# Queries and keys spread over partitions by DMA, and Newton inverse roots replaced by a power instruction on GpSimd, in a fused attention and expert layer

## The reference

```python
qg, kv = split_heads(ln(x) @ Wqg, 16), split_heads(ln(x) @ Wkv, 16)
queries, gates = qg[..., :16], qg[..., 16:]        # 16 key dims, 64 value dims per head
keys, values = kv[..., :16], kv[..., 16:]
queries, keys, values = l2norm(queries), l2norm(keys), l2norm(values)
attn = square(relu(queries @ keys^T))
out = tanh_norm(attn @ values) * tanh(silu(gates))
x = x + out @ Wout
x = x + moe(ln(x))      # 16 experts of 64, top 2 of 4 groups, top 4, and a shared expert
```

## Time and profile before

| what | value |
|---|---|
| median of the runs | 889.2 us |
| the profiled execution: its time, its span | 892.35 us, 890.6 us |
| PE busy | 753.3 us, 85% |
| DVE busy | 687.8 us, 77% |
| ACT busy | 512.4 us, 58% |
| POOL busy | 414.9 us, 47% |
| granted TensorE clock, mean | 0.944 |

### The profile page before, as it was taken

The page is one execution under the profiler, slowest core; times in us unless marked ns, Lnnn a source line. Parts: engine busy times, 40 slices in busy tenths (PEclk is TensorE's granted clock), DMA queues, the critical chain, the costliest instruction groups (busy, mean ns, idle before and its releaser), DMA issues.

```text
span 890.6 us, 17912 instructions
## 1 busy us (share of the span) xinstructions
PE 753.3 (85%) x5440; PEld 586.3 (66%) x5440; DVE 687.8 (77%) x2012; ACT 512.4 (58%) x1112; POOL 414.9 (47%) x395
## 2 busy tenths in 40 slices
PE   3787788889989888988988889898888898887876
PEld 2554557767766766766666677767677676765666
DVE  5767767888787878878788887878778887868654
ACT  4766466566656656666665666665665666643201
POOL 3474555464544645553455555445364645444000
PEclk9889799999999999999999999999999999999877
DMA  7000000000000000000000000000000000000000
GB/s 175 7 1 6 1 7 1 1 14 1 13 1 13 1 8 6 0 12 0 13 0 12 0 0 13 0 12 0 13 0 0 12 0 7 2 7 1 7 7 7
DMA packets 15988, 8.56 MB, mean 10 GB/s; under 512 B 5040, under 2 KB 15664, under 8 KB 15920
## 3 DMA queue, kind: packets, MB, share of 16 engines
q1 hardware_dynamic: 15920, 7.82, 3.3%
HBM read 5.72 MB, written 2.10 MB: 9 GB/s over the span
## 4 chain that ended last, share of the span: by engine, by line
PE 45%; DVE 42%; issue 8%; ACT 4%; POOL 1%; DVEq 1%; POOLq 0%; ACTq 0%
PE ps_a L464 8%; PE ps_f L328 7%; PE ps_f L330 5%; PE ps_f L329 5%; PE ps_f L408 5%; DVE norms_y L639 4%; DVE norms_t L638 4%; DVE ln_t L638 4%; PE ps_s L435 3%; PE ps_f L385 3%; DVE norms_t L637 3%; DVE it L850 3%; DVE it L832 3%; DVE ln_y L639 2%; DVE ln_t L637 2%
## 5 line engine op out<-in xcount | busy, mean ns | idle before, releaser
L295 POOL TENSOR_TENSOR p<-r 128x512 f32<-128x512 f32 x256 | 265.5, 1058 | 390.9 <-ACT r L577 390.9
L577 ACT ACTIVATE r<-ps_s 128x512 f32<-128x512 f32 x256 | 139.0, 599 | 37.2 <-PE ps_s L435 31.7
L464 PE MATMUL ps_a<-p,v 128*64 128x256 f32 x1024 | 147.3, 402 | 5.1 <-POOL p L295 4.5
L544 ACT ACTIVATE qkt<-ps_f 128x512 fp32r<-128x512 f32 x128 | 75.6, 599 | 42.9 <-PE ps_f L362 34.6
L569 ACT ACTIVATE it<-ps_f 128x256 f32<-128x256 f32 x144 | 56.1, 390 | 68.5 <-PE ps_f L330 66.8
L464 PEld LDWEIGHTS ps_a<-p,v 128*64 128x64 f32 x1024 | 64.7, 139 | 45.4 <-issue 6.4
L305 POOL TENSOR_TENSOR qks<-qk,qks 128x512 fp32r<-128x512 f32 x64 | 82.3, 1308 | 13.8 <-DVE qks L720 13.8
L832 DVE TENSOR_TENSOR it<-ps_f,it 128x256 f32<-128x256 f32 x144 | 58.7, 423 | 32.7 <-ACT it L569 25.4
L408 PE MATMUL ps_f<-wdown,it 128*128 128x128 f32 x576 | 75.7, 289 | 8.3 <-DVE it L850 8.3
L880 DVE TENSOR_TENSOR big<-ps_a,wt 128x256 f32<-128x256 f32 x128 | 52.1, 417 | 39.1 <-ACT big L586 27.4
L408 PEld LDWEIGHTS ps_f<-wdown,it 128*128 128x128 f32 x576 | 71.7, 204 | 15.2 <-issue 10.6
(11 more groups left out here) (152 smaller groups left out, 1732.3 us busy)
## 6 DMA issues: line engine op xcount, KB each, us to landing
x_in<-in_L_attn_tokens SPq DMA_DIRECT2D x16, 128.0 KB, 2.2
out<-o_sb SPq DMA_DIRECT2D x16, 128.0 KB, 1.8
big<-in_L_attn_Wqg SPq DMA_DIRECT2D x1, 640.0 KB, 3.8
big<-in_L_attn_Wkv SPq DMA_DIRECT2D x1, 640.0 KB, 5.1
big<-in_L_ffn_w_gate SPq DMA_DIRECT2D x1, 512.0 KB, 6.8
big<-in_L_ffn_w_up SPq DMA_DIRECT2D x1, 512.0 KB, 4.8
wout<-in_L_attn_Wout SPq DMA_DIRECT2D x1, 512.0 KB, 4.8
wdown<-in_L_ffn_w_down SPq DMA_DIRECT2D x1, 512.0 KB, 5.7
```

The costliest lines, as they stand in the source:

```text
L295: pool.tensor_tensor(p[h % 4][:], r[h % 2][:], r[h % 2][:], ALU.mult).then_inc(probs_done, 1)
L464: last = pe.matmul(ps_a[k % 2][64 * e:64 * e + 64, 0:N], v[q][:, t, h * DV:(h + 1) * DV], p[h % 4][:, t * N:(t + 1) * N], start=(t == 0), ...
L544: act.activation(qkt[pq][:, j, :], ps[:], ACT.Copy).then_inc(read[kind], 1)
L577: act.activation(r[h % 2][:], ps_s[h % 2][:], ACT.Relu).then_inc(relu_done, 1)
```

## The change

The transposes `tr`, the tile `qks` and its four writers are gone. The projections of queries and keys now have the weights as the stationary side, so that they come out transposed, with dims on partitions: 2 jobs of 2 x 3 matmuls with 256 columns in place of 2 jobs of 3 with 512. ScalarE writes their high part and their squares, VectorE their low part (`low_parts`, one instruction a job in place of L712 and L720), into `qk_parts` (1 MB). SyncE stores that tile to a DRAM buffer with one DMA, waits for it, and fills `qkt` (2 MB) with 12 loads, each of which writes 16 partitions; scores of pair 0 wait for all of them (`qk_loaded`). SyncE's steps are written out instead of looped over. The squares are summed per head by four more matmuls in the job `ones` (with `head16`), and `nT` turns 48 columns instead of 16; this replaces two of the six reductions L731. The last squares and sums of v (`sums(3)`) lie at the end of slot 1.

Both Newton roots become one instruction on GpSimd each, `tensor_tensor` with `ALU.pow` and an exponent tile of -0.5: for the norms, now 128 x 64, in slot 2 behind the pair's squares; for the layer norms, 128 x 4, in slot 6 behind the scaling of v. The inverse squares of query and key norms are VectorE reciprocals of 128 x 32. VectorE waits for the first root (`norms_ready`) ahead of `gate_up([5])`, and in slot 3 the order is head scales, value scales, `gate_up([6, 7])`, the gated heads, `gate_up([8])`. `FILL` is written anew. In step 17 `gate_up([0, 1, 2])` stands ahead of the route scores. GpSimd builds five more constant tiles or parts of them at the start.

```diff
-        [("P", "qk", 0), ("P", "qk", 1), ("P", "v", 0), ("O", "ones", 0), ("P", "v", 1), ("P", "v", 2)],
-        [("F", "gu", 0), ("P", "v", 3), ("O", "nT", 0), ("F", "lg", 0), ("F", "gu", 1), ("F", "gu", 2)],
-        [("F", "gu", 3), ("F", "gu", 4), ("F", "gu", 5), ("F", "gu", 6), ("F", "gu", 7)],
-        [("P", "g", 0), ("P", "g", 1), ("F", "gu", 8), ("P", "g", 2), ("O", "rT", 0)],
-        [("O", "rB", 0), ("P", "g", 3), ("O", "rB", 1), ("P", "tr", 0), ("O", "rB", 2), ("P", "tr", 1), ("O", "rB", 3),
-         ("P", "tr", 2)],
-        [("O", "y", 0), ("O", "y", 1), ("P", "tr", 3), ("F", "cT", 0), SKIP],
-        [("F", "cB", 0), ("P", "tr", 4), ("F", "cB", 1), ("P", "tr", 5), ("F", "cB", 2), ("P", "tr", 6), ("F", "cB", 3),
-         ("P", "tr", 7), SKIP],
+        [("P", "qk", 0), ("P", "v", 0), ("P", "qk", 1), ("P", "v", 1)],
+        [("F", "gu", 0), ("N", "ones", 0), ("P", "v", 2), ("F", "gu", 1), ("N", "nT", 0), ("P", "v", 3)],
+        [("F", "gu", 2), ("F", "lg", 0), ("F", "gu", 3), ("F", "gu", 4), ("F", "gu", 5)],
+        [("F", "gu", 6), ("F", "gu", 7), ("P", "g", 0), ("F", "gu", 8), ("O", "rT", 0)],
+        [("O", "rB", 0), ("P", "g", 1), ("O", "rB", 1), ("O", "rB", 2), ("P", "g", 2), ("O", "rB", 3)],
+        [("O", "y", 0), ("O", "y", 1), ("F", "cT", 0), SKIP],
+        [("F", "cB", 0), ("F", "cB", 1), ("P", "g", 3), ("F", "cB", 2), ("F", "cB", 3), SKIP],
...
+            def store_qk(b, q):
+
+                wait(sp, qk_loaded[q], (b - q) * (QK_LOADS // 2))
+                rows = qk_rows[q].rearrange("(l p) n -> p l n", p=P)
+                sp.dma_start(rows, qk_parts[:].rearrange("p l a c n -> p (l a c) n").bitcast(F32))\
+                  .then_inc(qk_stored[q], 16)
+
+            def load_qk(q):
+
+                rows = qk_rows[q].rearrange("(l a k e d) n -> l a e d k n", l=2, a=2, e=2, d=DK)
+                both = qk_rows[q].rearrange("(l m e d) n -> l e d m n", l=2, e=2, d=DK)
+                for e in range(2):
+                    for slot in range(4):
+                        at = 64 * e + DK * slot
+                        dst = qkt[q][at:at + DK, :, :, :].bitcast(F32)
+                        lq, lk = slot // 2, slot % 2
+                        if lq == lk:
+                            sp.dma_start(dst.rearrange("p a k n -> p (a k) n"), both[lq, e]).then_inc(qk_loaded[q], 16)
+                        else:
+                            sp.dma_start(dst[:, 0], rows[lq, 0, e]).then_inc(qk_loaded[q], 16)
+                            sp.dma_start(dst[:, 1], rows[lk, 1, e]).then_inc(qk_loaded[q], 16)
...
+                if "P" in on:
+                    b, pq = s + 1, 1 - q
+                    sp.wait_ge(read["qk"], 2 * b + 2)
+                    store_qk(b, pq)
+                    sp.wait_ge(qk_stored[pq], (b - pq) * 8 + 16)
+                    wait(sp, scores_done, 16 * (b - 1))
+                    load_qk(pq)
...
+            def root(tiles, ready):
+
+                y = tiles["y"][:]
+                pool.tensor_tensor(y, tiles["m"][:], minus_half[:].broadcast_to(y.shape), ALU.pow).then_inc(ready, 1)
+
+            def norm_roots(s, on):
+                if "P" in on:
+                    pool.wait_ge(sums_done, 4 * s + 8)
+                if "N" in on:
+                    pool.wait_ge(read["nT"], s + 2)
+                root(nt, norms_ready)
+
+            def ln_roots(s, on):
+                if "L" in on:
+                    pool.wait_ge(ch_l, 3 * (s + 3))
+                if "O" in on:
+                    pool.wait_ge(ch_n, 3 * s)
+                root(ln, ln_ready)
...
+                    if k == 2 and on & {"P", "O"}:
+                        norm_roots(s, on)
+                    if k == 6 and on & {"L", "O"}:
+                        ln_roots(s, on)
...
-                    last = three(ps[:, 0:2 * HK], (xh[:, tok[j]], xl[:, tok[j]]), (wqk[0][:], wqk[1][:]))
+                    for c in range(2):
+                        cols = slice(j * HK + c * P, j * HK + (c + 1) * P)
+                        last = three(ps[:, c * N:(c + 1) * N], (wqk[0][:, cols], wqk[1][:, cols]), (xh[:], xl[:]))
...
                 elif kind == "ones":
-                    pe.wait_ge(a2_done, 8 * b + 8)
-
-
-                    for a in range(2):
-                        for c in range(4):
-                            last = pe.matmul(ps[32 * c:32 * c + 32, 0:N], ones32[:, a, :], a2[:, 4 * a + c, :],
-                                             start=(a == 0), stop=(a == 1))
+
+                    sums = []
+                    if "O" in on:
+                        pe.wait_ge(a2_done, 8 * (s - 1) + 8)
+                        for a in range(2):
+                            sums.append([(ones32[:, a, :], a2[:, 4 * a + c, :]) for c in range(4)])
+                    if "P" in on:
+                        pe.wait_ge(qk_squared, 2 * (s + 1) + 2)
+                        sums.append([(head16[:], qk_sq[:, c // 2, c % 2, :]) for c in range(4)])
+                    for i, tiles in enumerate(sums):
+                        for c, (which, squared) in enumerate(tiles):
+                            last = pe.matmul(ps[32 * c:32 * c + 32, 0:N], which, squared,
+                                             start=(i == 0), stop=(i == len(sums) - 1))
...
-                    pe.wait_ge(read["tr"], 8 * b + 8)
+                    pe.wait_ge(qk_loaded[q], (b - q) * (QK_LOADS // 2) + QK_LOADS)
...
-                    act.activation(qk[:, j, :], ps[:, 0:2 * HK], ACT.Copy).then_inc(read[kind], 1)
+                    whole = ps[:].rearrange("p (c n) -> p c n", n=N)
+                    act.activation(qk_parts[:, 0, j, :, :], whole, ACT.Copy)
+                    wait(act, done["ones"], b)
+                    act.activation(qk_sq[:, j, :, :], whole, ACT.Square).then_inc(qk_squared, 1)
...
+            def low_parts(j, b):
+
+                dve.wait_ge(qk_squared, 2 * b + j + 1)
+                dve.tensor_tensor(qk_parts[:, 1, j, :, :], bank[("qk", j)][:].rearrange("p (c n) -> p c n", n=N),
+                                  qk_parts[:, 0, j, :, :].bitcast(F32), ALU.subtract).then_inc(read["qk"], 1)
...
                     if k == 2:
                         for c in range(3):
-                            if P_on or O:
-                                newton(link_norms, nt)
                             if F:
-                                gate_up([3 + c])
+                                gate_up([2 + c])
                             if c == 1:
                                 gated_heads(k)
-                        if F:
-                            gate_up([6])
+                        if P_on or O:
+                            dve.wait_ge(norms_ready, s + 2)
                         if O:
                             head_norms(link_o, b, rq2[pq])
                         if F:
-                            gate_up([7])
+                            gate_up([5])
                     if k == 3:
                         if O:
...
+                        if F:
+                            scale_hidden([0, 1, 2, 3])
                         if L_on or O:
-                            seed(link_ln, ln)
-                        if F:
-                            scale_hidden([0, 1])
-                        if L_on or O:
-                            newton(link_ln, ln)
-                        if F:
-                            scale_hidden([2, 3])
-                        if L_on or O:
-                            newton(link_ln, ln)
-                            newton(link_ln, ln)
-                            link_ln.end()
```

More of the change, by code:

```diff
@@ L258, in step @@
                       .then_inc(out_stored, 16)
-            run_steps(sp, step)
+            for s in range(FIRST_STEP, LAST_STEP + 1):
+                step(s, s % 2, stages(s), s)
             sp.wait_ge(out_stored, 16 * B)
@@ L297, in step @@
                         b = s + 1
-                        if k in (1, 2):
-                            t = k - 1
-                            wait(pool, done["tr"], 8 * b)
-                            for part in range(2):
-                                pool.wait_ge(qk_hi[t], 2 * b + part + 1)
-                                hi, lo, whole = slots_of(part, t)
-                                pool.tensor_tensor(lo, whole, hi.bitcast(F32), ALU.subtract).then_inc(qk_lo, 1)
                         if k in (4, 5, 6, 7):
@@ L495, in expert_weights @@
                 act.activation(weu[0][:], big[:, base + FC * P:base + 2 * FC * P], ACT.Copy).then_inc(w_hi, 1)
-            def high_parts(t, s):
-                b = s + 1
-                wait(act, done["tr"], 8 * b)
-                act.wait_ge(read["qk"], 2 * b + t + 1)
-                for part in range(2):
-                    hi, _, whole = slots_of(part, t)
-                    act.activation(hi, whole, ACT.Copy).then_inc(qk_hi[t], 1)
             def gates(j, s, q):
@@ L530, in evacuate @@
```

(34 more changed lines are left out.)

148 lines of the change are left out of this document (62 added, 86 removed).

## The result

The changed kernel takes 992.65 us (median of 4 runs, 991.79 to 993.01) where the kernel before takes 889.38 beside it (886.67 to 891.09): a ratio of 1.117, 95% interval 1.114 to 1.121. It is slower by 103 us. The forecast was 798.

A forecast was written before the change was run, and what follows sets the result against it. TensorE's own queue, interrupted by five waits, was taken to bound the full step: 51.1 us falling to 45.5, 73 us in 13 steps. With the other steps the sum was -91 us, 798 against 889.2; range 776 to 860.

The forecast's parts named there:

- I take 3 us for the norms (nearer the rows): GpSimd's power on 128 x 64 for the norm root: 3 us, chosen between estimates of 2.6 and 10.6.
- hidden up to 4.4 us: Norm root in slot 2: up to 4.4 us hidden before ScalarE's tanh; above that each microsecond costs one a step.
- `rT`: TensorE's wait at the end of slot 3, behind evacuation, tanh, scales and `gate_up` 6: a new wait of 2.2 us.
- `cT`: TensorE's wait for the routing chain: grows from 0.89 us by 1.1, as less TensorE work lies between.
- the term that was 0.5: Full step: 0.5 us added for the lower clock after waits of 2.2 and 2.0 us.
- the waits of the Newton rounds: Four TensorE waits for VectorE instructions behind Newton rounds: 4.9 us a full step go, and a slow stretch of 1.5.
- The round trip over DRAM: Store and loads of low parts and scores: 24 us taken, covered in full steps up to 38, visible in step -1.
- The 30 us: Round trip by the port rule, loads at 109 GB/s: 30 us, kernel 809 us; chance 0.14.
- 3.5 - 0.5 = 3.0 us a step: TensorE in a full step: removing eight `tr` jobs gives 3.5 us, four more `ones` matmuls cost 0.5.
- Rival (d): Waits only move, ScalarE late, `rT` and `cT` waiting at the lower clock: 2 us a step, 828 us; chance 0.07.
- rival (a): Root of 5 to 10 us shows, costing 0.6 to 5.6 us in each of 15 steps: 807 to 882; chance 0.13.
- (b): Root so slow that it decides: no gain from 10.5 us on, 972 us at 16; chance 0.06.

The follow-up runs named there:

- experiment 4: The changed kernel with the norm root cut into two halves of 32 columns, in slots 2 and 3, value scales formed in slot 4: 912.2 us.
- experiments 4 to 6: After experiment 4, the kernel of experiment 1 with the power on 24, then 40 of 64 norm columns, multiplication on the rest: 886.8 and 928.5 us.
- experiment 1: The changed kernel with the norm root replaced by a plain multiplication, norms left out of the result: 834.8 us.
- experiment 7: The kernel before with only the layer-norm root (4 columns) as a power on GpSimd behind slot 6: 850.6 us.
- experiment 9: Experiment 8's kernel with tanh behind `gu` 7, head and value scales between `gate_up` 6, 7 and 8, next x's row statistics behind the routing: 843.0 us.
- experiment 8: The changed kernel with the norm root back as Newton steps on VectorE, the layer-norm root kept as a power: 854.8 us.
- 10: Experiment 1's kernel with the three moves of experiment 9 and `g` 3 ahead of `cT`: 817.0 us.
- 12: Experiment 9's kernel with `g` 3 ahead of `cT`, routing scores behind `scale_heads`, and the Newton seed in one instruction: 821.2 us.

## Why the prediction was wrong

The step that failed is "I take 3 us for the norms (nearer the rows)": the power took 10.5 us. Its companion "hidden up to 4.4 us" failed too: the cover was 2.2. The rest of the sum is judged beside them.

**The price.** Measured: 1.01 us for 4 columns, 4.16 for 24, 5.42 for 32, 6.74 for 40, 10.52 for 64, 20.73 for 128. That is a line of 0.16 us for each element of a partition and 0.4 fixed, so 77 plain operations of 2.07 ns for each element, and the prediction's own upper end (80 operations, 10.6 us). Between ends of 0.25 and 10.6 us that no row told apart it chose the one next to the plain rows and gave the other 0.13 and 0.06. The Trainium skill (GPSIMD Engine Reference, Performance versus the Vector engine), at about half VectorE's speed for elementwise work, describes the plain operations and not this one. In this trace GpSimd's square of 128 x 512 takes 1.04 us and VectorE's product of the same size (L853, one input in PSUM) 0.69, so the plain gap is 1.5 here.

**The cover.** The prediction measured the room up to the tanh, whose result `rT` needs. The tanh was due just when it said, 9.4 us after the scores of pair 2 (450.37). But VectorE waits in order, and `gate_up` 5 stands behind `norms_ready`; TensorE needs its bank for `gu` 8 at 449.67, 5.0 us after the root begins. The prediction counted this bank rule for `rT` and `gate_up` 6, and not for `gu` 8 and `gate_up` 5. The measured cover is 2.2 us, three times over (experiments 4 to 6). It also overlooked that the head norms come right when GpSimd squares the pair that it held back, so that two instructions of 0.2 us take 1.0 each; it had this very stretch in the earlier trace rows. That is the larger half: as an estimate, with 0.4 us for the two instead of 2.0 the cover would have been 3.8 us.

**The full step, term by term.** Forecast 45.5 us, measured 56.7 in the step shown, 11.2 more: the wait for `gate_up` +8.3, `rT` -2.0 (0.23 where 2.2 was forecast, for `gate_up` 6 now follows a longer wait), `cT` +0.9 (2.93 for 2.0, with two of the routing's small instructions at 1 us beside GpSimd), `xT` +0.8, which no term held, and TensorE busy for 44.5 where 41.3 was implied (41.7 less the wait of 0.89, and 0.5 for the clock), +3.2. The last is the lower clock, the term that was 0.5. In experiment 1, where the root costs nothing, the picture fits better, with 2.4 us too little in the sum: 47.9 for 45.5, with TensorE busy for 41.6, `rT` 2.55, `cT` 2.94, `xT` 0.76. So the waits of the Newton rounds go as forecast and the two new waits are where they were said to be, but both were taken too small and `xT` was left out. Even with a root of 0.3 us the kernel would have stood at 834.8, 37 us above the forecast, and 13 x 2.4 = 31 of these lie in the full steps.

**The whole.** The span is 991.1 where 800 was forecast: 13 x 11.6 = 150 in full steps, 27 in steps 0 and 1 (95.9 for 69), 2.6 ahead of them, 13.6 in steps 15 and 16 (85.2 for 71.6, the same root in them), -2.3 in the last. Together 191.

**The round trip over DRAM** came out at the time forecast, in part by luck. In the same step SyncE issues the store at 436.22 and the first load at 440.64; the DMA view of 430 to 487 in slices of 1.43 us shows the loads to end near 459:

```profile
DMA  0500099199999999999970000000000000000000
GB/s 18 166 0 6 1 343 346 45 183 104 114 119 101 119 109 110 116 104 117 113 65 0 0 0 0 0 0 0 0 0 0 0 6 0 0 0 0 0 0 0
```

That is 23 us from issue to end, where 24 was taken, and no full step waits for it. But the 24 was a value between two sums and neither sum is what happened: the loads took 18.7 us with their landing, where the sum at full rate had 8.5 and 2.2, and the store 4.4 instead of 4.2 and 2.2. In step -1 it shows as forecast (45.6 us to the first scores for 43; with the root out of the way, in experiment 1, 13.4 us of it are a wait for the loads):

```profile
46.24 0.80 PE L485 MATMUL ps_s<-qkt 64*128 64x256 f32 x4 [13.39 <-DMA qkt<-qk_rows]
```

The loads run at 101 to 119 GB/s, the store at 345. The Trainium skill's rule (SBUF — State Buffer, Door 1: The DMA port swizzle), by which a block of 16 partitions reaches 4 of 16 ports, gave 109 GB/s and 19 us for the loads; the trace agrees, 18.7 us. The 30 us that followed from it for the whole round trip did not come, it was 23. That the ports are the cause of the rate wasn't tried.

**What taking the transpositions off TensorE is worth.** The prediction counted 3.5 - 0.5 = 3.0 us a step. At a granted clock of 1.00 in both, TensorE is busy for 43.4 us in a step with them (experiment 7) and 41.2 without (experiment 9):

```profile
457.40:505.50 48.10, 43.41 (x341) 34.15 (x341) 39.00 (x111) 31.59 (x69) 26.61 (x25) 1.00 0.02 6
```

```profile
462.30:509.90 47.60, 41.17 (x322) 31.38 (x322) 37.46 (x108) 26.93 (x62) 21.36 (x21) 1.00 0.50 72
```

So 2.2 us, and in the order of the change all of it came back. Without `tr` as cover, `cT` waits 2.9 us instead of 0.9 and `rT` 1.7 instead of nothing (experiment 8 against 7): TensorE's waits go from 4.8 to 6.6 us a step on average over ten, and the clock from 1.00 in the step shown to 0.93 and 0.96 in two steps of experiment 8. Rival (d), "waits only move", describes the rest of the change well: it put the kernel at 828 with 2 us more a step, and experiment 1 is at 834.8 with 2.4. What the root alone cost is rival (a) by mechanism, at a length where (b) drew its line: 10.5 us was called the point of no gain, and the measured 10.5 us gave +12%. With a cover of 2.2 the same sum would have put that point near 8; the runs put it at 4.4 us.

Experiments 10 and 12 are close (817.0 with a root that costs nothing and the old place of the routing scores, 821.2 with Newton and the new one) because their full steps are the same, 46.6 us on average over ten, with 4.3 and 4.4 us of waits. In 10, 2.2 of them stand at the bank of `rB` 0; in 12 that wait is gone, and 1.9 stand at `cT` and 0.9 at `gate_up`.

What stays open: the three moves were tried only in the layout with the DMA. Whether they would give as much with the transpositions on TensorE, and so whether the DMA is worth anything once the order is right, isn't known. Whether the root as a multiplication gains from the new place too wasn't run. Newton steps on GpSimd weren't tried.

## What to carry to other kernels

A single instruction can take as long as dozens of others of its form: when no row prices it, the high end of the bound belongs in the forecast with real weight, and here a power cost 77 times a plain operation for each element. Use such an instruction where few elements need it: for 4 columns it cost 1 us of an idle engine and took eleven dependent VectorE instructions off the end of the step, 4%, and for 64 it cost 158 us against a root that takes no time. The cover of a wait ends at the first thing queued behind it on the waiting engine that someone else needs, not at the reader of the result. Small instructions behind the wait count at their length beside a busy neighbour, not at their length alone. Before taking fillers off TensorE, look at which chains they cover: the removal alone gave nothing, and the moves in the order after it gave 34 us (854.8 to 821.2, the shorter seed among them).

## What the runs showed of the hardware

A power on GpSimd takes 0.16 us for each element of a partition, as long for 128 columns (20.73 us) as 20 plain instructions of 512. Beside GpSimd's squares, VectorE instructions of 128 x 32 with both inputs in SBUF that take 0.2 us alone took about 1.0 (L757 and L758 above, L760 and L761 in experiment 4). Beside the power one of them kept its length (L776, 0.18 us in experiment 4).

The granted clock was 0.50 behind the wait of 8.3 us. Behind short waits their length did not decide it. In experiment 9 the same wait for `rB` 0 was followed by 1.00 in one step (2.20 us, window 492.5 to 497.5) and by 0.67 in the next (2.25 us, window 540.1 to 545.1). Behind `gate_up` waits of 1.2 and 1.8 us it was 0.66 in the kernel before and 1.00 in experiment 7. With 24 columns, behind waits of 2.15 and 1.28 us, it was 0.64 in the 5 us from 458 on.
